# Masked attention: another order of the query tiles, and a scaling of the output per pair of tiles

## The reference

```python
def _temporal_experts(xt, idx, qw, qb, kw, kb, vw, vb, pw, pb):
    B, T, _ = xt.shape
    q = (jnp.einsum('btd,bod->bto', xt, qw[idx]) + qb[idx][:, None, :]).reshape(B, T, H, HD)
    k = (jnp.einsum('btd,bod->bto', xt, kw[idx]) + kb[idx][:, None, :]).reshape(B, T, H, HD)
    v = (jnp.einsum('btd,bod->bto', xt, vw[idx]) + vb[idx][:, None, :]).reshape(B, T, H, HD)
    logits = jnp.einsum('bthd,bshd->bhts', q, k) * HD ** (-0.5)
    causal = jnp.tril(jnp.ones((T, T), dtype=bool))
    logits = jnp.where(causal, logits, -jnp.inf)
    att = jax.nn.softmax(logits, axis=-1)
    o = jnp.einsum('bhts,bshd->bthd', att, v).reshape(B, T, D)
    o = jnp.einsum('btd,bod->bto', o, pw[idx]) + pb[idx][:, None, :]
    return xt + o
```

## Time and profile before

| | us |
|---|---|
| median of 3 runs | 3441.09 (3441.07 to 3444.06) |
| the profiled execution | 3439.76 |
| its span, first to last instruction | 3437.5 |
| masked attention, first to last exponential | 2056.23 to 2289.61 |
| TensorE busy over the span | 2854.2 (83%) |
| VectorE busy | 1925.7 (56%) |
| ScalarE busy | 1457.2 (42%) |
| GpSimd busy | 1115.2 (32%) |

### The profile page before, as it was taken

One profiled execution on the slowest core, in us unless ns is written; L12 is line 12 of the kernel. 1 busy time (PEld: TensorE's weight loads), 2 busy tenths in 40 slices (PEclk: granted clock), 3 DMA queues, 4 the chain that ended last, 5 costly groups with the idle time before them and its releaser, 6 DMA issues. The chain is left out here.

```text
span 3437.5 us, 46642 instructions
## 1 busy us (share of the span) xinstructions
PE 2854.2 (83%) x15398; PEld 1999.1 (58%) x15398; DVE 1925.7 (56%) x3890; ACT 1457.2 (42%) x3150; POOL 1115.2 (32%) x1138
## 2 busy tenths in 40 slices
PE   0403887999958995779999798989999999998899
PEld 0201227777756763434444585558777687776687
DVE  7203774577642114579999526653677636776544
ACT  0100003466604542556666435542566435665322
POOL 4777775467113433076665000000000000001220
PEclk9856998999968997989999899999999999999999
DMA  4104775533156994454443264214423044321322
GB/s 109 36 6 114 210 202 160 138 61 72 40 161 212 339 341 125 162 172 150 138 136 92 79 191 107 56 58 129 129 54 67 15 146 113 73 48 41 98 75 87
DMA packets 228769, 407.93 MB, mean 119 GB/s; under 512 B 48706, under 2 KB 146288, under 8 KB 224438
## 3 DMA queue, kind: packets, MB, share of 16 engines
q1 hardware_dynamic: 173222, 268.49, 27.3%
q0 software_dynamic: 54864, 136.39, 14.8%
q10 hardware_dynamic: 448, 0.08, 0.0%
HBM read 318.32 MB, written 90.35 MB: 119 GB/s over the span
## 5 line engine op out<-in xcount | busy, mean ns | idle before, releaser
L904 ACT ACTIVATE at_p<-at_pb,at_max 125x1250 f32<-125x1250 f32 (+4 forms) x320 | 383.8, 1199 | 302.0 <-DVE at_unused L975 273.3
L790 PE MATMUL at_pb<-ident,at_p 125*125 125x125 f32 x2880 | 433.6, 281 | 20.8 <-ACT at_p L904 17.6
L790 PEld LDWEIGHTS at_pb<-ident,at_p 125*125 125x125 f32 x2880 | 391.2, 191 | 83.7 <-ACT at_p L904 22.0
L807 PE MATMUL at_pb<-at_pt,at_v 125*64 125x250 f32 x2880 | 355.3, 383 | 5.2 <-DVE s_t L1008 3.0
L1457 PE MATMUL so_ps<-g_got,g_hot 128*125 128x512 f32 x332 | 177.5, 630 | 204.8 <-DMA g_got<-support,g_edges 172.0
L968 DVE TENSOR_REDUCE at_wide<-at_pb 125x1 f32<-125x1024 f32 x240 | 293.6, 1223 | 22.1 <-PE at_pb L773 3.8
L890 ACT ACTIVATE at_pt<-at_pb 125x500 f32<-125x500 f32 (+1 forms) x448 | 232.8, 520 | 97.4 <-PE at_pb L790 93.5
L712 POOL TENSOR_TENSOR s_t<-s_t,at_all 128x500 f32<-128x500 f32 (+1 forms) x33 | 42.7, 1293 | 656.2 <-DVE s_t L1008 656.0
L807 PEld LDWEIGHTS at_pb<-at_pt,at_v 125*64 125x64 f32 x2880 | 188.2, 137 | 104.1 <-issue 14.4
L750 PE MATMUL at_pb<-at_s,at_shared 128*128 128x500 f32 (+1 forms) x1152 | 229.2, 361 | 23.2 <-ACT at_shared L852 23.2
L986 DVE COPY at_pt<-at_pb 125x500 f32<-125x500 f32 (+1 forms) x416 | 232.4, 582 | 22.6 <-PE at_pb L790 22.6
(11 more groups left out here) (320 smaller groups left out, 5505.7 us busy)
## 6 DMA issues: line engine op xcount, KB each, us to landing
w_ring<-in_L_ffn_w SPq DMA_DIRECT2D x128, 512.0 KB, 11.7
at_shared<-k_parts SPq DMA_DIRECT2D x64, 312.5 KB
ml_w<-in_mlp_w SPq DMA_DIRECT2D x64, 256.0 KB
k_parts<-at_shared SPq DMA_DIRECT2D x64, 250.0 KB, 2.9
q_parts<-at_shared SPq DMA_DIRECT2D x64, 250.0 KB, 3.4
h_edges<-em_both SPq DMA_DIRECT2D x11, 1024.0 KB, 3.9
g_h<-h_edges SPq DMA_DIRECT2D x11, 1024.0 KB, 5.6
at_shared<-q_parts SPq DMA_DIRECT2D x32, 312.5 KB
```

Of the source, the lines that this page charges most:

```text
L790: ins = pe.transpose(pturn[0:TN, g % 2, TN * (t % 4):TN * (t % 4) + TN], p[:, u % 2, TN * t:TN * t + TN], c.ident[0:TN, 0:TN])
L807: ins = pe.matmul(pout[side:side + 64, 0:2 * TN], v[:, t, 2 * j + h, :], p_t[:, q % 2, t, :], start=(t < 2), stop=(t >= keys[u] - 2))
L904: act.activation(p[:, t % 2, 0:w], score[t % 2][0:TN, 0:w], ACT.Exp, bias=neg_max[:, t:t + 1], accum_out=total[:, t:t + 1]).then_inc(exp_d ...
```

## The change

The pairs of query tiles of the masked attention are taken in the order m = 8, 0, 6, 2, 4, which is 10, 2, 8, 4, 6 keys, where they were taken in the order 0, 2, 4, 6, 8. Each pair of tiles is a group of its own for the scaling, so there are five groups for each pair of heads, 20 in all. The attentions without a mask keep their order and their three groups. The scratch tensor in DRAM for the reciprocals has 20 rows for 12.

```diff
--- before.py
+++ after.py
@@ -590,7 +590,9 @@
         pieces = [[(0, 512), (512, 1024), (1024, N)], [(TAIL, TAIL + 512), (TAIL + 512, N), (0, TAIL)]]
 
         w_out = k_hi_both[:, :, :].rearrange("p h n -> p (h n)")[:, 0:DC * D].rearrange("p (k d) -> p k d", k=DC)
-        units = [(j, h, i) for j in range(PAIRS_) for m in range(0, NT, 2) for h in range(2) for i in (m, m + 1)]
+        groups = [(8,), (0,), (6,), (2,), (4,)] if causal else [(0, 2), (4, 6), (8,)]
+        order = [m for g in groups for m in g]
+        units = [(j, h, i) for j in range(PAIRS_) for m in order for h in range(2) for i in (m, m + 1)]
         keys = [(i // 2 * 2 + 2 if causal else NT) for _, _, i in units]
         turns = [-(-n // 4) for n in keys]
         upto = lambda u: sum(turns[:u])
@@ -607,8 +609,10 @@
             if dve_by(g):
                 eng.wait_ge(dve_took, dve_by(g))
 
-        norms = [(j, k) for j in range(PAIRS_) for k in range(3)]
-        n_units = lambda j, k: (UNITS * j + 8 * k, UNITS * j + min(8 * k + 8, UNITS))
+        norms = [(j, k) for j in range(PAIRS_) for k in range(len(groups))]
+        until = lambda k: sum(len(g) for g in groups[:k])
+        n_units = lambda j, k: (UNITS * j + 4 * until(k), UNITS * j + 4 * until(k + 1))
+        n_columns = lambda k: (TN * groups[k][0], TN * (groups[k][-1] + 2))
         with stage(nc, "bias_in", "bias_set", "s_high", "s_low", "w_in0", "w_in1", "w_high", "w_low", "summed", "high",
                    "low", "saved", "first_in", "kq_in0", "kq_in1", "scored", "wide_scored", "wide_ready", "masked", "max_ready", "exp_done",
                    "turned", "act_took", "dve_took", "pv_done", "half_out", "added", "inv_made", "inv_out", "inv_in",
@@ -704,9 +708,9 @@
 
                 def scale(x):
                     j, k = norms[x]
-                    lo, hi = CHUNKS[k]
+                    lo, hi = n_columns(k)
                     pool.wait_ge(inv_in, 32 * (x + 1))
-                    pool.wait_ge(added, NT * j + min(4 * k + 4, NT))
+                    pool.wait_ge(added, NT * j + 2 * until(k + 1))
                     dst = out_t[:, j, lo:hi].rearrange("q (i p) -> q i p", p=TN)
                     by = inverse_all[:, 0:hi - lo].rearrange("q (p i) -> q i p", p=TN)
                     pool.tensor_tensor(dst, dst, by, ALU.mult).then_inc(scaled, 1)
@@ -2361,7 +2365,7 @@
         support, x1, z2 = (rows(n) for n in ("support", "x1", "z2"))
         y_moe = dram("y_moe", [EXPERTS, CAP, D])
         scratch = (dram("q_parts", [2, HEADS // 2, 128, N]), dram("k_parts", [2, HEADS // 2, 128, N]),
-                   dram("inverse", [3 * HEADS // 2, 2, 4 * TN]), dram("w_out", [128, DC, D]))
+                   dram("inverse", [NT // 2 * HEADS // 2, 2, 4 * TN]), dram("w_out", [128, DC, D]))
         hold = lambda: nc.sbuf_tensor(f"x_sb_{nc.next_id()}", [TN, NT, D], F32, side="right")
         with ExitStack() as layer0:
             s0 = lambda name, shape, dt=F32: layer0.enter_context(nc.sbuf_tensor(name, shape, dt))
```

## The result

| | before | changed |
|---|---|---|
| median, us | 3440.8 (20 runs, 3431.85 to 3444.06) | 3446.7 (20 runs, 3442.58 to 3451.33) |
| ratio | | 1.0021, 95% interval 1.0014 to 1.0027 |
| the profiled execution, us | 3439.76 | 3448.77 |
| its span, us | 3437.5 | 3447.0 |
| first to last exponential, us | 233.38 | 238.82 |

The changed kernel is slower: by 5.9 us between the medians, by 7.2 by the ratio, whose interval gives 4.8 to 9.3. That is about the 0.2% which the prediction named as the limit of this measurement, but the interval does not reach down to no change. The forecast was 5.2 us.

A forecast was written before the change was run, and what follows sets the result against it. No engine is full; a chain between exponentials across engines bounds the loop, lengthened by products with V and TensorE's clock. Terms 2.79 + 4.64 - 1.23 + 1.04 - 2.06 = +5.2 us on 3441.1 gave 3446.3, range 3437 to 3452.

The forecast's parts named there:

- Step 10 to 2: First head pair's 2-key group now also follows 10-key units, 10.32 us instead of 7.53: +2.79 us.
- Step 8 to 4: 4-key groups: products of 8-key units lengthen both long gaps, while the clock no longer falls: +4.64 us in all.
- One predecessor fewer for the 10-key group: The 10-key group follows another group three times, not four, saving one costly first gap: -1.23 us.
- Opening: Loop's start: the first unit has 10 keys, its maximum takes 1.46 us instead of 0.42: +1.04 us.
- End of the loop: Last unit has 6 keys instead of 10; last reciprocal comes sooner, the way to the last scaling stays 6.60: -2.06 us.
- Scaling per pair of tiles: 20 reciprocals, DRAM trips and GpSimd multiplications of 250 columns instead of 12 groups: costed at nothing.
- The free step: Rival for the 4-key groups: 8-key product finishes before the awaited exponential, 8.96 us go, 3437.3 us; chance 0.12.
- the filling: Rival in the loop: small units fill the large ones' gaps on TensorE, time could reach 3426 us; chance 0.04.
- The late trips: Rival on the scalings' DRAM trips: they fall behind and the loop's end slips by about 2, 3448.3 us; chance 0.05.
- The clock falls: Rival behind the 2-key groups: TensorE's clock falls in the new order too, losing 4.32 us, 3450.6 us; chance 0.21.

The follow-up runs named there:

- one_step: The changed kernel with its order set to 10, 2, 4, 6, 8 keys; ratio to the kernel before 1.0012 (1.0003 to 1.0021).
- last_small: Changed kernel with order 2, 6, 8, 10, 4 keys and the product's last quarter ahead of the score piece in odd 2- and 4-key units; ratio 0.9975.
- pv_first_new: Changed kernel with the last quarter of the product with V ahead of the gated score piece in odd 2- and 4-key units; ratio 0.9995.

## Why the prediction was right, point by point

- **Step 10 to 2** (+2.79). Measured +3.31 for the 2-key groups. The first pair's went from 7.52 to 10.49, and 7.52 was at a clock of 0.58. The 0.52 over the forecast are in the main four times 0.12: the last gap of the group is 1.87 with 8-key units behind it and was 1.75.
- **Step 8 to 4** (+4.64). The gap was put together from six rows as 3.68 and is 3.68, in all eight places. The group came out at 11.56, not 11.74. The mis-sized part is the base of 9.5 for a group without the step at full clock. In the old order that base is 9.60; in the changed one it is 9.32, as with the filler, because the product of the 8-key units keeps TensorE from the long idle: its transposes start 0.06 after the exponential's end, where they started 0.36 after it, which the prediction did not have. Measured +3.92, and this comes out as three prices: four times 2.24 for the product, +8.96; the falls of the kernel before, 42.32 less four times 9.60, -3.92 for the 4.32 forecast; and the earlier start, four times 0.28, -1.12.
- **One predecessor fewer for the 10-key group** (-1.23). The gap into a 10-key group is 3.80 after 6 keys, 3.77 after 8, as assumed. The 6-, 8- and 10-key groups together moved by -5.07 + 1.02 + 2.26 = -1.79. Of the 0.56 over the forecast, 0.43 are the opening group, 14.15 where one inside the loop takes 14.58; in the two later traces of this order it took 14.88, so this gain came in one execution of three.
- **Opening** (+1.04). From the first unit's mask to its exponential 0.96 before (2055.27 to 2056.23) and 2.00 now (2055.23 to 2057.23): +1.04. The mask itself stands behind the last projection, which comes when DMAs end, and wanders from execution to execution.
- **End of the loop** (-2.06). Measured -2.04 to the reciprocal, but the trip took 0.44 more. That it "stays 6.60" was the weak word: over these kernels it took 6.5 to 8.2.
- **Scaling per pair of tiles** (nothing). Confirmed by the five scalings in the old order, 1.0004. The changed kernel's last scaling waited for its own trip, not for GpSimd.
- **The sum** (+5.2). The stage gave +4.84 in the first pair of traces and 5.0 to 6.1 over all, the difference of the medians is +5.9, the ratio's interval 4.8 to 9.3. Whether the 1 to 3 us between the stage and the three ratios lie in other stages stays open.

The signs that the prediction named came: 3.68 with the product between piece and mask, a first 2-key group of 10.49, a first pair of 60.37 us, a clock of 1.00 behind the opening, the reciprocal 2.32 after the last exponential.

The rivals. The free step is refuted by the 3.68, the filling by 2-key groups that still take 10.43 to 10.49. The late trips are refuted by the end of the loop. The clock falls did not return in the changed order's small groups, in three profiled executions, only at its opening at +0.73, a sixth of that rival's price; they do return in other orders (one_step, last_small), so the rival was a real one. Over all traces the clock stood at 1.00 in 16 of 16 4-key groups that have 8-key units ahead of them (pv_first_new counted in) and below 0.9 in 13 of 20 that stand behind the 2-key units without filler. That the 8-key units between shut the rival out follows from these counts; what in them does it was not tested.

By the luck of errors that cancel, the total of this pair of traces is nearer than the terms: the 4-key group 0.7 less, the 2-key group 0.5 more, the large groups 0.6 less, the trip 0.4 more.

## What to carry to other kernels

Where an in-order engine waits for a gate, look at what is queued behind the gated instruction and is part of the next link of the chain; moving that ahead of the gate was worth about 9 us in the changed order and 4.5 in the old one, where the change of the order by itself cost 6 to 8. Whether the order of last_small would gain without it was not run. An order of tiles is to be judged by which unit's leftovers fall into which unit's chain, and by where it leaves TensorE thin, not by how evenly the sizes go. An engine that idles ahead of a gate can also cost by a late start and a lower clock; here eight matmuls without a use were cheaper than both. And when two orders differ by 0.2%, ask of the trace whether the clock fell in that execution, before a gain or a loss is given to the order.

## What the runs showed of the hardware

- Eight matmuls of 250 columns without a use, ahead of each odd 4-key unit, went with a clock of 1.00 in the three groups that had 0.71, 0.68 and 0.84, and made the kernel 5.2 us faster (2.1 to 8.2). In two executions with the filler none of eight 4-key groups had a fall, in four without it 9 of 16.
- Behind an idle of 0.2 to 1.24 us TensorE's transposes started 0.05 to 0.06 us after the end of the exponential they waited for, behind one of 1.39 to 1.62 us 0.26 to 0.40 after it, in all thirteen traces. Where the clock had just fallen or was falling, the late start also stood behind idles of 0.77 to 0.92 us, so the length of the idle alone does not decide it.
- The same order of TensorE's instructions had falls of the clock in the 4-key groups of all four pairs in one execution, of three in another and of one in a third; the group took 9.6 us without and 10.2 to 11.9 with.
- The clock fell without a long wait of TensorE: busy 10.39 of 11.26 us at 0.60 in the third pair of the five scalings, 6.76 of 9.58 at 1.00 in the second, and in the 2-key group ahead of either the longest idle before a transpose was 1.6 us. The Trainium skill, "TensorE: Matmul & The Clock Gate", section "Loop structure matters more than you think", says that the loop nest decides whether matmuls stay at the full clock, and names long waits for DMA as what loses it. Here the order alone did decide it in part (no fall in the changed kernel's small groups, falls in one_step's), but these runs show falls with waits of no such kind, and an order that falls in one execution and not in the next.
- From the last reciprocal to the last scaling, the trip through DRAM and back, it took from 6.5 to 8.2 us over the profiled executions, with the same two DMAs. What sets it was not looked into.
